# Narrower tap tiles and a one-sided low product in the convolution of a conv + GRU kernel

## The reference, cut to what matters

```
def conv(x, w, b):          # depthwise causal, K = 128 taps, one tap row per channel
    y[b, t, d] = sum_k w[k, d] * x[b, t + k - (K - 1), d]      # x is 0 before t = 0
    return y + b

def gru(h0, x):             # 64 steps
    gi = x[:, t] @ W_ih + b_ih ;  gh = h @ W_hh + b_hh
    r, z = sigmoid(i_r + h_r), sigmoid(i_z + h_z)
    n = tanh(i_n + r * h_n)
    h = (1 - z) * n + z * h

x = x + conv(x, cond, b0)   # x: (128, 64, 512), cond: (128, 512) is both the taps and h0
x = x + gru(cond, x)
```

## Time and profile before

| | |
|---|---|
| time, median of 3 | 1240.26 us (1236.8 to 1242.55) |
| span of the profiled execution (the only time that the page gives of it) | 1237.5 us |
| PE busy | 1182.9 us, 96% |
| DVE, ACT, POOL busy | 539.3, 500.2, 17.2 us |
| TensorE's granted clock, mean | 0.991 of full speed |
| DMA | 97.98 MB in 288354 packets, 79 GB/s over the span |

### The profile page before, as it was taken

The page is one execution under the profiler, slowest core; times in us unless marked ns, Lnnn a source line. Parts: engine busy times, 40 slices in busy tenths (PEclk is TensorE's granted clock), DMA queues, the critical chain, the costliest instruction groups (busy, mean ns, idle before and its releaser), DMA issues.

```text
span 1237.5 us, 15341 instructions
## 1 busy us (share of the span) xinstructions
PE 1182.9 (96%) x5518; PEld 986.4 (80%) x5518; DVE 539.3 (44%) x811; ACT 500.2 (40%) x934; POOL 17.2 (1%) x19
## 2 busy tenths in 40 slices
PE   1997999899989999999999999999999999999997
PEld 1976788787878888888888888888888888888886
DVE  2835766476655333333333333333333333333333
ACT  4436766576755333323333323333332333332332
POOL 0400000000000000000000000000000000000000
PEclk9999999899989999999999999999999999999999
DMA  9978888788853111111011111001111101111100
GB/s 244 293 176 161 167 173 175 170 183 174 173 149 77 54 32 35 34 34 32 24 29 34 34 34 34 25 25 34 34 34 34 28 24 34 34 34 34 32 17 21
DMA packets 288354, 97.98 MB, mean 79 GB/s; under 512 B 212752, under 2 KB 282384, under 8 KB 286272
## 3 DMA queue, kind: packets, MB, share of 16 engines
q1 hardware_dynamic: 283968, 96.29, 33.1%
q10 hardware_dynamic: 4352, 1.25, 0.4%
HBM read 63.34 MB, written 34.14 MB: 79 GB/s over the span
## 4 chain that ended last, share of the span: by engine, by line
PE 89%; ACT 3%; issue 2%; SPq 2%; DMA 2%; DVE 2%; ACTq 0%; DVEq 0%
PE bank L779 80%; PE bank L801 4%; PE bank L741 2%; PE bank L768 2%; SPq L347 1%; ACT tmp L561 1%; ACT x_parts L551 1%; SPq L358 1%; DMA early<-early_result 1%; ACT bank L519 0%; ACT toep_early L500 0%; DMA xres<-stage 0%; DVE stage L679 0%; DVE x_parts L668 0%; DMA tap_pad<-tap_rows 0%
## 5 line engine op out<-in xcount | busy, mean ns | idle before, releaser
L779 PE MATMUL bank<-w_ih_hi,xT_hi 128*128 128x512 f32 x768 | 308.2, 401 | 0.0
L779 PE MATMUL bank<-w_ih_hi,xT_lo 128*128 128x512 f32 x768 | 302.2, 394 | 0.0
L779 PE MATMUL bank<-w_ih_lo,xT_hi 128*128 128x512 f32 x768 | 302.2, 393 | 0.0
L779 PE MATMUL bank<-w_hh_hi,hT_hi 128*128 128x512 f32 x768 | 299.6, 390 | 0.0
L779 PE MATMUL bank<-w_hh_lo,hT_hi 128*128 128x512 f32 x768 | 299.5, 390 | 0.0
L779 PE MATMUL bank<-w_hh_hi,hT_lo 128*128 128x512 f32 x768 | 298.8, 389 | 0.0
L779 PEld LDWEIGHTS bank<-w_ih_hi,xT_lo 128*128 128x128 f32 x768 | 145.6, 190 | 31.8
L779 PEld LDWEIGHTS bank<-w_hh_hi,hT_lo 128*128 128x128 f32 x768 | 144.2, 188 | 30.4
L779 PEld LDWEIGHTS bank<-w_ih_hi,xT_hi 128*128 128x128 f32 x768 | 146.1, 190 | 27.2 <-ACT bank L519 0.4
L779 PEld LDWEIGHTS bank<-w_ih_lo,xT_hi 128*128 128x128 f32 x768 | 146.1, 190 | 26.8
L779 PEld LDWEIGHTS bank<-w_hh_hi,hT_hi 128*128 128x128 f32 x768 | 144.4, 188 | 28.1
(11 more groups left out here) (59 smaller groups left out, 802.3 us busy)
## 6 DMA issues: line engine op xcount, KB each, us to landing
x_unit<-in_x_dram SPq DMA_DIRECT2D x64, 256.0 KB, 4.7
toep_ring<-kernel_parts SPq DMA_DIRECT2D x128, 128.0 KB, 3.3
out_dram<-outZ SPq DMA_DIRECT2D x256, 64.0 KB, 1.6
xres<-stage SPq DMA_DIRECT2D x32, 384.0 KB, 5.0
xT<-xres SPq DMA_DIRECT2D x192, 64.0 KB, 1.9
early<-early_result SPq DMA_DIRECT2D x4, 1024.0 KB, 13.8
xT<-early SPq DMA_DIRECT2D x60, 64.0 KB, 2.0
w_ih_raw<-in_L_cond_W_ih_dram SPq DMA_DIRECT2D x12, 256.0 KB, 7.8
```

Source lines behind the costliest of these rows:

```text
L779: mm = nc.tensor.matmul(psum[:, :], a[:, rows], b[w][:, cols], start=False, stop=stop and n == 2, skip_group_check=True)
```

## The change

The 48 stored output times alone are computed: a tap tile has 96 columns (two times 48) in place of 128, a channel's loads are 48 long in place of 64, and PSUM, `tmp`, `stage` and `bias_pair` are used on 96 partitions, with the second channel at partition 48. The product with the low taps takes only the 128 columns of x_hi; so low taps times x_lo is no longer added. The number of instructions on each engine, their order and their waits stay. Each slot of the ring is shorter, while the ring's size, and so POOL's clearing, stays.

```diff
-    TOEP = 2 * BLOCK * P
-    toep_ring = place("toep_ring", T_RING * TOEP, F32R)
+    TOEP = 2 * BLOCK * 2 * LATE
+    toep_ring = place("toep_ring", T_RING * 2 * BLOCK * P, F32R)
...
-                    source = bass.AP(first.tensor, first.offset, [[1, T], [P, 2 * BLOCK], [1, T]])
+                    source = bass.AP(first.tensor, first.offset, [[1, T], [P, 2 * BLOCK], [1, LATE]])
                     sp.dma_start(
                         toep[j % T_RING][c * T:(c + 1) * T].bitcast(F32).rearrange(
-                            "s (n e) -> s n e", e=P)[:, :, c * T:(c + 1) * T],
+                            "s (n e) -> s n e", e=2 * LATE)[:, :, c * LATE:(c + 1) * LATE],
...
-                                 stage[n % 2][c * T:c * T + LATE, :]).then_inc(stage_stored[n % 2], 16)
+                                 stage[n % 2][c * LATE:(c + 1) * LATE, :]).then_inc(stage_stored[n % 2], 16)
...
-                    nc.scalar.activation(tmp[m % 2][:, pair * B:(pair + 1) * B],
-                                         conv_bank[m % 3][:, pair * 2 * B:pair * 2 * B + B], ACT.Identity,
-                                         bias=bias_pair[:, 2 * m + pair:2 * m + pair + 1]).then_inc(tmp_ready, 1)
+                    nc.scalar.activation(tmp[m % 2][0:2 * LATE, pair * B:(pair + 1) * B],
+                                         conv_bank[m % 3][0:2 * LATE, pair * 2 * B:pair * 2 * B + B], ACT.Identity,
+                                         bias=bias_pair[0:2 * LATE, 2 * m + pair:2 * m + pair + 1]).then_inc(tmp_ready, 1)
...
-                    stage[s % 2][:, at:at + 2 * B].rearrange("p (g b) -> p g b", b=B),
+                    stage[s % 2][0:2 * LATE, at:at + 2 * B].rearrange("p (g b) -> p g b", b=B),
...
                     for low in range(2):
-                        at = (slot * 2 + low) * P
-                        mm = nc.tensor.matmul(conv_bank[m % 3][:, pair * 2 * B:(pair + 1) * 2 * B],
-                                              toep[j % T_RING][:, at:at + P],
-                                              parts[j % HL_RING][:, slot * 2 * B:(slot + 1) * 2 * B],
-                                              start=low == 0, stop=low == 1)
+                        at = (slot * 2 + low) * 2 * LATE
+                        late = toep[j % T_RING][:, at:at + 2 * LATE]
+                        cols = B if low else 2 * B
+                        mm = nc.tensor.matmul(conv_bank[m % 3][0:2 * LATE, pair * 2 * B:pair * 2 * B + cols], late,
+                                              parts[j % HL_RING][:, slot * 2 * B:slot * 2 * B + cols],
+                                              start=low == 0, stop=low == 1, skip_group_check=True)
```

More of the change, by code:

```diff
@@ L480, in _ @@
                 first = conv_b[c * UNIT:(c + 1) * UNIT]
-                act.dma_start(bias_pair[c * T:(c + 1) * T, :].rearrange("s (n g) -> s n g", g=UNIT),
-                              bass.AP(first.tensor, first.offset, [[0, T], [2 * UNIT, NUNIT], [1, UNIT]])
+                act.dma_start(bias_pair[c * LATE:(c + 1) * LATE, :].rearrange("s (n g) -> s n g", g=UNIT),
+                              bass.AP(first.tensor, first.offset, [[0, LATE], [2 * UNIT, NUNIT], [1, UNIT]])
                               ).then_inc(conv_bias_loaded, 16)
@@ L679, in second_half @@
                 nc.vector.tensor_tensor(
-                    stage[s % 2][:, at:at + 2 * B].rearrange("p (g b) -> p g b", b=B),
-                    conv_bank[m % 3][:, :].rearrange("p (g l b) -> p g l b", l=2, b=B)[:, :, 1, :],
-                    tmp[m % 2][:, :].rearrange("p (g b) -> p g b", b=B),
+                    stage[s % 2][0:2 * LATE, at:at + 2 * B].rearrange("p (g b) -> p g b", b=B),
+                    conv_bank[m % 3][0:2 * LATE, :].rearrange("p (g l b) -> p g l b", l=2, b=B)[:, :, 1, :],
+                    tmp[m % 2][0:2 * LATE, :].rearrange("p (g b) -> p g b", b=B),
                     ALU.add).then_inc(stage_ready, 1)
```

## The result

The changed kernel takes 1230.0 us (median of 4, 1228.8 to 1230.91) beside 1241.18 for the kernel before: ratio 0.9919, 95% interval 0.9898 to 0.9939. A second series beside the experiments gave 1228.45 us, ratio 0.9912 (0.9894 to 0.993). Forecast were 1232.7, in a range of 1224 to 1260. The span of the profiled execution went from 1237.5 to 1228.7 us. In a profile of the second series the same changed kernel has a span of 1221.1 us, so a few us read from one profile each show no difference between two kernels; the times and the length of undisturbed steps do.

The account below looks back on a forecast made before the run. PE was taken as the bound, with loads nearly full beside it from 112 to 345 us; 6.1 us from the low product plus 1.5 from tap loads made 7.6 us less, 1232.7 us as a median, range 1224 to 1260.

Parts of the forecast that it names:

- What bounds the kernel: Before 395 us everything is decided: PE and loads nearly full from 112 to 345 us, then PE alone.
- The low product's own cost: L801's 256 low products: 0.0825 us before a 96-column load, 0.11 before the gates' 128-column load, in place of 0.12.
- the transposes' row: Transposes at L741, 128 columns moving and 128 loaded for each, 0.11 us: the basis for pricing the low product.
- That saves ... 6.1 us: Low products at L801: 4.8 us from the first of each bank plus 1.3 from the second, all counted as time saved.
- the gain is waited away: Rival, crowded stage: waits for late loads grow by what banks saved, leaving 1.1 us, 1239 us; chance 0.10.
- The sign that was named for this rival: PE's idle time in the crowded stage: well above 13 us would mean the gain is waited away.
- I take 1.5 us gained, close to nothing: Tap loads at L358, 96 KB in place of 128: late loads come less late, 1.5 us gained.
- The bound of 13.4 us of idle time: PE's idle time from 112 to 345 us, the most that shorter tap loads could gain.
- The stage stores move the same 48 rows from other partitions: nothing: Stage stores: the same rows taken from other partitions, claimed to change the time by nothing.
- The f32 rate: Rival, 256 low products at L801: 0.222 in place of 0.12 us each, 1254 us, slower; chance 0.36.
- columns alone: Rival, low products at L801: cost goes by moving columns only, 16.9 us saved, 1223 us; chance 0.08.
- ACT and DVE: L561 and L679 on fewer partitions keep 364 and 418 ns; if shorter, it would not show.

Follow-up runs that it names:

- the 64-column load: The changed kernel with only the first 64 of a tap tile's 96 columns loaded into PE as stationary operand: 1228.61 us, ratio 0.991 to the kernel before.
- the kernel with the full low product: The changed kernel with its low product back at 256 moving columns, 96-column tiles, loads and stores kept: 1228.87 us, ratio 0.9918 to the kernel before.
- the next halving: The changed kernel with tap loads of 24 output times in place of 48, 48 KB per DMA: 1223.75 us, ratio 0.9881 to the kernel before.
- the run that moved only them on top: The kernel before with short tap loads and moved stage stores, plus ACT's and DVE's evacuation on 96 partitions: 1232.67 us, ratio 0.9938.

## Why the prediction was right in its number and wrong in its parts

- *What bounds the kernel*: right. Nothing moved from 395 us on but the start (a plain step 16.79 and 16.80), and all 8.9 us of the profiled spans lie in the bulk.
- *The low product's own cost*: right as a sum. 0.0825 and 0.11 us, a bank of 0.43 and a step of 21.3 were forecast; the trace has 0.38 + 0.05 and 21.30, and the 64-column load gave 21.04 for 21.05. Taking the transposes' row and scaling it by the columns loaded behind the product was the right choice between ends of 0.06 and 0.222. The transposes understate a 128-column fp32r load a little: two of them in a bank left the step at 21.69, so some 0.116 rather than 0.11, by the forecast's 0.12 for a wide product. The product before the 96-column load is then some 0.077 in place of 0.0825: two small errors that cancel.
- *"That saves ... 6.1 us"*: this step failed. 6.0 us are there in the undisturbed steps, but with and without the narrow product the kernel takes the same time (0.9912 and 0.9919 with it, 0.9918 without). The rival "the gain is waited away" had the mechanism: in the crowded stretch PE meets SP's queue at each late load, and what PE saved ahead of it is waited for. Its counter-argument was that SP gets earlier with PE. Between the kernel before and the change SP did, by 4.6 us at the bank of the earlier trace rows, but there the loads had shrunk too; with short loads in both kernels, PE was 2.0 us earlier at that bank and SP 0.4. The sign that was named for this rival, idle time well above 13 us, didn't appear (11.0 and 8.3), because the shorter loads cut the waits at the same time; the kernel with the full low product, at 8.5, is what it had to be held against, and one profile of each doesn't separate them. The rival had 0.10, and alone it would have given 1239.
- *"I take 1.5 us gained, close to nothing"* for the tap loads: mis-sized. The bytes alone are worth 3.6 us and, at the next halving, 3.5 to 4.7 more. The bound of 13.4 us of idle time did hold it. One of the two reasons given for so little was weak: the tap loads of the crowded stretch are the smaller part of the traffic, but at 97 x 128 KB they are 12.4 MB and x's 12.3. That a late load costs by what it holds up, and not by its share of the bytes, fits the runs but wasn't tested apart.
- *"The stage stores move the same 48 rows from other partitions: nothing"*: wrong, 2.8 us alone and 5 us beside the short loads. Short loads and moved stores together give 0.993, the tiles 0.9918, with overlapping intervals; whether a rest of 1 to 2 us is there, and what it is, stays open.
- *The f32 rate* for short fp32r products (0.36): refuted by all products of 128 columns here; *columns alone* (0.08): refuted by the 21.69 us.
- *ACT and DVE*: right. L561 and L679 took 355 and 413 ns on 96 partitions, where 364 and 418 were kept, and the run that moved only them on top gained nothing.

So 7.6 us were forecast, out of 6.1 and 1.5, and some 10 came out of about none and all. The time came near the forecast because the two errors had opposite signs: that is luck, and the number doesn't bear the sum out.

## What to carry to other kernels

Where an engine and a DMA queue are both nearly full, price an edit against the queue first: of a busy engine's saving nothing may arrive (here less than some 4 of 6 us), while a quarter off the loads that it waits for may (here 3.6 us). Compare such an engine with and without the edit at the same late load, and look at what the other queue does meanwhile. In these runs a matmul of few moving columns cost what the load behind it costs, so narrow the stationary operand with the moving one or leave both. Test the parts of a change apart even when the sum fits, since a right sum proves none of its terms.

## What the runs showed of the hardware that was not expected

- A product of 128 fp32r columns runs at the same rate per column as the wide ones, about 0.06 us, where its neighbours' loads leave it room: with 64-column loads a bank's four products take 0.35 us on the chain, 2 x 0.12 + 2 x 0.055 if the wide ones keep their 0.12 (an estimate).
- Stage stores of the same size and number from partitions 0 to 95, in place of 0 to 47 and 64 to 111, made the kernel 0.23% faster (0.9977, 0.9966 to 0.9988) with nothing else changed.
- A wait cost more than its length. Behind a wait of 3.09 us PE's granted clock over 2 us was 0.51, the 1.2 GHz level, and a gate product took 0.43 us from start to start; behind one of 1.57 us at the same bank the clock was 1.00 (2.4 GHz) and the product took 0.23.
